# Typed attention pass of a graph network: one-hots on ScalarE, type masks built once, the next group's scores split around the totals

## The reference, cut to what matters

```python
k = typed_linear(x, Wk, bk); q = typed_linear(x, Wq, bq); v = typed_linear(x, Wv, bv)   # by node type, 4 heads
k_rel = einsum('nhd,rhde->rnhe', k, rel_att)      # 6 edge types
v_rel = einsum('nhd,rhde->rnhe', v, rel_msg)
att = (q[edge_dst] * k_rel[edge_type, edge_src]).sum(-1) * rel_pri[edge_type] / sqrt(dk)
seg = edge_dst * 6 + edge_type                    # a softmax for each destination and type
ex  = exp(att - segment_max(att, seg)[seg])
w   = ex / segment_sum(ex, seg)[seg]
hsum = segment_sum(w[:, :, None] * v_rel[edge_type, edge_src], seg)
```

## Time and profile before

| | |
|---|---|
| median of 3 runs | 8833.31 us (8825.69 to 8842.84) |
| profiled execution, span | 8830.1 us |
| mean granted TensorE clock over the span | 0.819 |
| TensorE matmul, busy | 6600.0 us (75%) |
| VectorE | 5164.4 us (58%) |
| GpSimd | 4060.3 us (46%) |
| ScalarE | 2234.7 us (25%) |
| typed pass, from 592 to 2110 us | 1518 us, of it VectorE 1309.29, TensorE 1098.34, GpSimd 817.01, ScalarE 353.68 |

### The profile page before, as it was taken

How to read it: one execution, slowest core, us unless ns; L and a number is a source line. 1 busy time by engine, 2 the same in 40 slices (tenths; PEclk the granted TensorE clock), 3 DMA queues, 4 the chain that set the end, 5 groups by cost and what they waited for, 6 DMA issues and landing times. The chain is left out here.

```text
span 8830.1 us, 116392 instructions
## 1 busy us (share of the span) xinstructions
PE 6600.0 (75%) x27378; PEld 5018.6 (57%) x27379; DVE 5164.4 (58%) x9644; ACT 2234.7 (25%) x4857; POOL 4060.3 (46%) x4373
## 2 busy tenths in 40 slices
PE   4977777774736666679999999974788885787886
PEld 2546566563525444546666666653676673666665
DVE  3138888886243333246666666665666666566666
ACT  1222222221310000123333333332333331333332
POOL 0025555552037777124444444423666661666663
PEclk9988888886857777589999999986777776677777
DMA  2247767666013333133343344332444441544443
GB/s 92 99 144 212 214 208 213 207 209 151 4 57 105 105 105 105 29 108 115 115 124 114 116 121 116 117 83 85 135 139 135 131 140 37 149 133 135 136 135 90
DMA packets 440058, 1096.42 MB, mean 124 GB/s; under 512 B 102452, under 2 KB 177296, under 8 KB 439410
## 3 DMA queue, kind: packets, MB, share of 16 engines
q0 software_dynamic: 249344, 763.23, 30.9%
q1 hardware_dynamic: 190180, 328.60, 11.1%
HBM read 1009.55 MB, written 81.94 MB: 124 GB/s over the span
## 5 line engine op out<-in xcount | busy, mean ns | idle before, releaser
L731 POOL DMA_INDIRECT st_rows<-g_table,st_stage_idx x1632 | 1558.0, 955 | 873.4 <-issue 463.6
L824 POOL DMA_INDIRECT st_rows<-kv_table,st_stage_idx x832 | 806.2, 969 | 671.1 <-PE st_psM L1167 391.2
L2385 PE MATMUL st_psM<-st_msg,st_hot 128*128 128x273 f32 x3264 | 942.6, 449 | 128.0 <-DVE st_msg L2233 102.6
L677 POOL DMA_INDIRECT st_rows<-p_table,st_stage_idx x816 | 854.3, 1047 | 302.9 <-issue 220.3
L731 POOL DMA_INDIRECT st_rows<-h_table,st_stage_idx x816 | 777.0, 952 | 244.5 <-issue 234.8
L2385 PEld LDWEIGHTS st_psM<-st_msg,st_hot 128*128 128x128 f32 x3264 | 702.9, 221 | 321.5 <-DVE st_msg L2233 91.2
L1519 DVE TENSOR_TENSOR st_pre<-st_psP,st_rows 128x512 f32<-128x512 f32 x816 | 523.5, 682 | 531.5 <-PE st_psP L1610 392.6
L1616 PE MATMUL st_psC<-st_w,st_rT 128*128 128x256 f32 x3264 | 814.7, 392 | 0.0
L1616 PEld LDWEIGHTS st_psC<-st_w,st_rT 128*128 128x128 f32 x3264 | 587.3, 190 | 373.7 <-ACT st_rT L1577 212.3
L1426 PE MATMUL st_psM<-st_rows,st_hot 128*128 128x256 f32 x1632 | 512.3, 484 | 372.5 <-DMA st_rows<-h_table,st_stage_idx 190.4
L1426 PEld LDWEIGHTS st_psM<-st_rows,st_hot 128*128 128x128 f32 x1632 | 401.3, 251 | 480.7 <-issue 331.3
(11 more groups left out here) (394 smaller groups left out, 11250.1 us busy)
## 6 DMA issues: line engine op xcount, KB each, us to landing
st_dst_row<-in_dst_row SPq DMA_DIRECT2D x310, 512.0 KB, 5.7
kv_table<-st_rows_out SPq DMA_DIRECT2D x25, 1560.0 KB, 5.7
st_ea<-in_ea SPq DMA_DIRECT2D x103, 256.0 KB, 3.8
st_rows<-g_table,st_stage_idx POOLq DMA_INDIRECT x1632, 2.8
st_pens<-pen_table SPq DMA_DIRECT2D x208, 72.0 KB
st_rows<-kv_table,st_stage_idx POOLq DMA_INDIRECT x832, 4.5
st_rows<-h_table,st_stage_idx POOLq DMA_INDIRECT x816, 2.7
st_rows<-p_table,st_stage_idx POOLq DMA_INDIRECT x816, 3.7
```

The lines of the kernel that those rows point to most:

```text
L677: pool.indirect_dma_start(out=rows[:, u * SLOTS + j, :], out_offset=None, in_=table, in_offset=bass.IndirectOffsetOnAxis(ap=stage_idx[:, u ...
L731: pool.indirect_dma_start(out=rows[:, slot, j, :], out_offset=None, in_=table, in_offset=bass.IndirectOffsetOnAxis(ap=stage_idx[:, g, u * ...
L824: pool.indirect_dma_start(out=rows[:, slot, j, :], out_offset=None, in_=kv_table, in_offset=bass.IndirectOffsetOnAxis(ap=stage_idx[:, g, u ...
L2385: last = nc.tensor.matmul(out[:, 0:MSG_W], onehots[:, j, :], msg[:, n, j, :], start=(j == 0), stop=(j == SLOTS - 1))
```

## The change

In the typed pass:

- `make_hot` moves from VectorE to ScalarE. It becomes, for each supertile, eight Squares of 128 columns (iota row plus a bias of minus the destination number, `minus_rel`), a wait for them, and one Relu of 1,024 columns. Its place is behind `make_extra_hotrows(q + 1, 1)`, ahead of `make_hotrow(q + 2, .)`.
- `mine` and `other` are made once for all slots, as 16-bit floats, in `typed_tables`, behind the preparation of the relation weights. `spread_types` keeps its four additions.
- `edge_scores(q + 1, 0)` is split: the first half of the slots comes between the maxima and the totals, the second behind the totals.
- `extra_hots` comes behind the messages.
- Both work tables hold 16-bit numbers; `prepare` writes `minus_rel` in one more instruction; some tiles move to other scopes; in `typed_tables` the type masks are made ahead of two fills.

```diff
@@ gnn
-    work = sb(top, "work", [1, NS + 2 * U + 2, 4], I32)
+    work = sb(top, "work", [1, NS + 2 * U + 2, 4], U16)
...
-    type_f = sb(early, "type_f", [P, NT + UT * SLOTS])
-    typed_rel = sb(early, "typed_rel", [P, NT])
-    typed_work = sb(early, "typed_work", [1, NS + 2 * U + 2, 4], I32)
+    minus_rel = sb(early, "minus_rel", [P, NT])
+    mine = sb(early, "mine", [P, NT + UT * SLOTS, RELS], BF16)
+    other = sb(early, "other", [P, NT + UT * SLOTS, RELS], BF16)
+    typed_work = sb(early, "typed_work", [1, NS + 2 * U + 2, 4], U16)
@@ prepare
+                    v.tensor_scalar(minus_rel[:, :], typed_rel[:, :], -1.0, None, ALU.mult)
@@ typed_tables, VectorE
+                    link.turn()
+                    wide = [P, NT + UT * SLOTS, RELS]
+                    link(v.tensor_tensor(mine[:, :, :], type_f[:, :].unsqueeze(2).to_broadcast(wide),
+                                         iota_row[:, 0:RELS].unsqueeze(1).to_broadcast(wide), ALU.is_equal))
+                    link(v.tensor_scalar(other[:, :, :], mine[:, :, :], -1.0, BIG, ALU.add, ALU.mult))
@@ typed_pass, VectorE
-                    def edge_scores(q, u, slot, turn):
+                    def edge_scores(q, u, slot, turn, halves=(0, 1)):
                         s = UT * q + u
-                        _, x1, _, _ = work_typed(dve, s + 1)
-                        typed_rows_in(dve, slot, turn)
-                        for h in range(2):
+                        if 0 in halves:
+                            _, x1, _, _ = work_typed(dve, s + 1)
+                            typed_rows_in(dve, slot, turn)
+                        for h in halves:
...
                     def spread_types(q):
-                        link(v.tensor_tensor(mine[:, :, :, :, :].rearrange("p u k j r -> p (u k j) r"),
...
-                        link(v.tensor_scalar(other[:, :, :, :, :], mine[:, :, :, :, :], -1.0, BIG, ALU.add, ALU.mult))
...
-                                    other[:, u, half, :, :].unsqueeze(2).to_broadcast(wide),
+                                    types_of(other, q, u, half),
...
                         link.turn()
-                        make_hot(q, 0)
                         segment_maxima(q)
-                        make_hot(q, 1)
+                        edge_scores(q + 1, 0, ahead_slot, ahead_turn, (0,))
                         segment_totals(q)
-                        edge_scores(q + 1, 0, ahead_slot, ahead_turn)
+                        edge_scores(q + 1, 0, ahead_slot, ahead_turn, (1,))
                         edge_weights(q)
                         for u in range(UT):
                             messages(slot + u, u)
+                        for u in range(UT):
+                            extra_hots(q, u)
                         link(edge_scores(q + 1, 1, ahead_slot + 1, ahead_turn))
                         spread_types(q + 1)
-                        for u in range(UT):
-                            extra_hots(q, u)
@@ typed_pass, ScalarE
+                    def make_hot(q, u):
+                        s = UT * q + u
+                        link.turn()
+                        act.wait_ge(S["summed"], START + s - 1)
+                        for j in range(SLOTS):
+                            last = nc.scalar.activation(hot[:, u, j, :], iota_row[:, :], ACT.Square,
+                                                        bias=minus_rel[:, ds(s * SLOTS + j, 1)])
+                        link(last)
+                        nc.scalar.activation(hot[:, u, :, :], hot[:, u, :, :], ACT.Relu, bias=ones_col[:, :],
+                                             scale=-1.0).then_inc(S["onehot"], 1)
...
                         make_extra_hotrows(q + 1, 1)
+                        for u in range(UT):
+                            make_hot(q, u)
                         for u in range(UT):
                             make_hotrow(q + 2, u, 16 * q + 48)
```

More of the change, by code:

```diff
@@ L22 @@
 I32 = mybir.dt.int32
+U16 = mybir.dt.uint16
 ALU = mybir.AluOpType
@@ L174, in gnn @@
     hidden = ExitStack()
+    type_f = sb(hidden, "type_f", [P, NT + UT * SLOTS])
     X = sb(hidden, "x_in", [P, NB, D])
@@ L196, in prepare @@
             first = st.sb("first", [P, NT])
+            typed_rel = st.sb("typed_rel", [P, NT])
             least = st.sb("least", [P, 2, NS])
@@ L593, in _ @@
                     link = Link(dve, S["link_dve"])
-                    link(v.memset(rows[:, :, 2 * D:KV_W], 0.0))
-                    for r in range(RELS):
-                        v.memset(rows[:, r, 2 * D + r:2 * D + r + 1], 1.0)
                     for t in range(TYPES):
@@ L602, in _ @@
                     last.then_inc(S["masks"], 1)
+                    link(v.memset(rows[:, :, 2 * D:KV_W], 0.0))
+                    for r in range(RELS):
+                        v.memset(rows[:, r, 2 * D + r:2 * D + r + 1], 1.0)
                     dve.wait_ge(S["rel_in"], 16 * 3 * H0)
@@ L774, in typed_pass @@
             att = st.sb("att", [P, UT, 2, HALF, H0])
-            mine = st.sb("mine", [P, UT, 2, HALF, RELS])
-            other = st.sb("other", [P, UT, 2, HALF, RELS])
             et = st.sb("et", [P, HALF, 2, UT, G])
@@ L789, in typed_pass, with types_of @@
             psM = [st.ps(f"psM{u}", [P, 512]) for u in range(UT)]
-            columns = psM[0][:, 512 - P:512]
+            def types_of(tile, q, u, half):
+                return tile[:, ds((UT * q + u) * SLOTS + half * HALF, HALF), :].unsqueeze(2).to_broadcast([P, HALF, H0, RELS])
             lanes = psX[0:T_LANES, :]
@@ L956, in spread_types @@
                     def spread_types(q):
-                        link(v.tensor_tensor(mine[:, :, :, :, :].rearrange("p u k j r -> p (u k j) r"),
-                                             type_f[:, ds(UT * q * SLOTS, UT * SLOTS)].unsqueeze(2).to_broadcast([P, UT * SLOTS, RELS]),
-                                             iota_row[:, 0:RELS].unsqueeze(1).to_broadcast([P, UT * SLOTS, RELS]), ALU.is_equal))
-                        link(v.tensor_scalar(other[:, :, :, :, :], mine[:, :, :, :, :], -1.0, BIG, ALU.add, ALU.mult))
                         wide = [P, HALF, H0, RELS]
@@ L965, in spread_types @@
                                     et[:, :, half, u, :].rearrange("p j (h r) -> p j h r", h=H0),
-                                    other[:, u, half, :, :].unsqueeze(2).to_broadcast(wide),
+                                    types_of(other, q, u, half),
                                     att[:, u, half, :, :].unsqueeze(3).to_broadcast(wide), ALU.add)
                         last.then_inc(S["scored"], 1)
-                    def make_hot(q, u):
-                        s = UT * q + u
-                        x0, _, _, _ = work_typed(dve, UT * q + 1)
-                        dve.wait_ge(S["summed"], START + s - 1)
-                        dve.wait_ge(S["opened"], START + UT * q - 1)
-                        dve.wait_ge(S["x_opened"], START + x0)
-                        one_hot(hot[:, u, :, :], typed_rel[:, ds(s * SLOTS, SLOTS)], columns).then_inc(S["onehot"], 1)
                     def extra_hots(q, u):
@@ L982, in extra_hots @@
                         with dve.If(more):
-                            link(v.tensor_copy(rel[:, :], typed_rel[:, ds(s * SLOTS, SLOTS)]))
+                            link(v.tensor_scalar(rel[:, :], minus_rel[:, ds(s * SLOTS, SLOTS)], -1.0, None, ALU.mult))
                             with dve.Fori(x0, x1) as x:
@@ L1021, in edge_weights @@
                                     totals[:, :, half, u, :].rearrange("p j (h r) -> p j h r", h=H0),
-                                    mine[:, u, half, :, :].unsqueeze(2).to_broadcast(wide),
+                                    types_of(mine, q, u, half),
                                     back_view()[:, :, at:at + G].rearrange("p j (h r) -> p j h r", h=H0), ALU.mult)
@@ L1051, in group @@
                             messages(slot + u, u)
+                        for u in range(UT):
+                            extra_hots(q, u)
                         link(edge_scores(q + 1, 1, ahead_slot + 1, ahead_turn))
                         spread_types(q + 1)
-                        for u in range(UT):
-                            extra_hots(q, u)
-                    v.tensor_copy(columns, iota_row[:, :])
                     link(v.tensor_reduce(pick[:, :], ident[0:T_LANES, 0:T_LANES].rearrange("p (c r) -> p c r", r=RELS),
```

## The result

The changed kernel takes 8856.47 us (median of 10 runs, 8843.46 to 8879.99), the kernel before 8833.05 in as many. The ratio is 1.0029, with a 95% interval of 1.0019 to 1.0038: slower by some 23 us, where 8707 was forecast. The profiled execution has a span of 8855.8 us, 25.7 more than before.

What follows compares the result with a forecast made beforehand. VectorE was taken to set the pace in the typed pass, with TensorE a close second. 50 groups times (29.05 - 26.5) gave 127 us, less 0.6, from the median 8833.3 to 8707; range 8645 to 8775.

Steps and rivals of the forecast that it cites:

- Part 5: GpSimd needs 21.1 us a group and fits; masks hidden; 16-bit loads taken at the same time, 16 us either way.
- Rival D: 16-bit row takes one load per number: 1.03 us more a read, later stages +245, typed pass +75, 9027 us; chance 0.05.
- Part 1: What leaves VectorE: scan starts at 0.95 us instead of 3.09, gain 2.1, second L715 1.14; register work hidden behind messages.
- Part 2: VectorE's new order in the typed pass: new 1.3 us wait ahead of L1020; VectorE alone gives 25.9 us a group.
- Part 3: TensorE's low-clock expansion holds the sums back 0.8 to 1.6 us, adding 0.3 to 1.1; 26.5 us a group taken.
- Rival A: The forecast: VectorE and TensorE set the pace by turns, 26.2 to 27.0 us a group, 8680 to 8735; chance 0.60.
- Part 4: ScalarE: a Square of 128 columns takes 0.3 us, one make_hot 3.7 us, ready before TensorE needs it; costs nothing.

Runs made afterwards that it cites:

- e1: The changed kernel with both work tables back at 32-bit numbers and the first two numbers of a row masked with 4095: 8709.37 us, ratio 0.9858.
- e2: The kernel before with both work tables of 16-bit numbers and nothing else: 9167.73 us, ratio 1.0377.
- e9: Reads alone, nothing of the network computed, twelve of each kind: on VectorE four 16-bit numbers took 0.945 us, four 32-bit ones 0.339.
- e11: e1 with half of the products of TensorE's expansion of (q+1, 1) left out: 8758.66 us, ratio 0.992.
- e3: The kernel before, 32-bit tables kept, with the first two numbers of each row read masked with 4095: 8902.60 us, ratio 1.008.
- e10: e1 with the mask made only where a number is used, and at the read on SyncE alone: 8685.78 us, ratio 0.9835.
- e6: The same kernel as e10, run on another chip where the kernel before takes 10386.75 us: ratio 1.007.

## Why the prediction was wrong

**The step that failed** is in Part 5: "No row shows a 16-bit load. I take the same time", with a tenth either way for its bounds. The read takes 2.76 times as long, 0.948 against 0.344 us. A price that no row showed was bounded by a tenth of its nearest row, though VectorE alone pays it 476 times outside the typed pass. Rival D had the place and almost the form: one load per number, 1.03 us more. The load stays one instruction and costs 0.60 more. Put through D's own sum: 238 exposed reads times 0.60 is 143 us (measured 126), and behind the messages 2.2 + 3 x 0.60 = 4.0 us fit under 4.53, so that only the bare one counts, 30 us in 50 groups (after less e1: 0.62 a group, 31). That gives 8707 + 143 + 30 = 8880, 24 over the measured 8856. The half that D took as exposed came near as a total only: VectorE's read is bare in all 102 supertiles of the edge network and costs nothing in the weighted sum. D's chance, 0.05, was too low. e1, e2 and e9 settle the cause: the type alone, put in or taken out, moves the edge network, the attention passes and the typed pass, and the read by itself has the same length. That e1, the change with its reads at the old price, takes 8709 us where 8707 was forecast is luck in part: its typed pass gained 138 us and its attention passes 30, its edge network and typed tables lost 51.

**Part 1: right.** The table loads of the extra ranges cost nothing behind the messages.

**Part 2: right, with one term missing.** Gap ahead of L1020 1.30 us, forecast 1.3. L999 stands 1.05 us behind the additions in e1 (1443.95 + 0.77 to 1445.77), forecast 0.95; in after 1.29. Missing is the bare read ahead of the first half of the scores: 0.72 us of gap a group with 16-bit reads, 0.22 with 32-bit ones (e1, masks and all). Part 1 rightly let VectorE's sequencer run four instructions ahead behind the messages. Between maxima and totals it can't, because it has just waited for the end of L1000. The trace of before shows the same read bare behind the totals (0.60 us ahead of L950, rows 3).

**Part 3: the mechanism right, its size too large.** The clock still falls, and TensorE's gap was 5.76 us in after and 4.88 in e1 (4.7 forecast). With 16-bit reads the sums are held 1.2 us. In e1 the low stretches are 6.8, 10.2 and 10.2 us long in turn, and in such three groups the sums start 2.58, 3.00 and 3.63 us after the messages, held 0.0, 0.4 and 1.1 us. The first and the last of them:

```profile
1436.99 7.33 PE L1178 MATMUL st_psM<-st_rows,st_hot 128*128 128x262 f32 x32
1444.87 0.61 PE L1203 MATMUL st_psX<-ident,st_et 128*96 128x128 f32 x4 [0.55 <-DVE st_et L972]
...
1490.37 7.23 PE L1178 MATMUL st_psM<-st_rows,st_hot 128*128 128x262 f32 x32
1497.43 0.60 PE L1203 MATMUL st_psX<-ident,st_et 128*96 128x128 f32 x4
```

In the first TensorE is done 0.55 us before VectorE's additions and delays nothing; in the last, held by a full 1.1 us, it starts them 0.4 us after the additions' end at 1497.05. The forecast let a hold of 0.8 to 1.6 us come in every group and pass on 0.3 to 1.1 of it. What passes on is bounded by L999's idle time, 1.10 us a group where 0.95 is bare latency: 0.15. With 25.9 us of VectorE alone, 26.22 leaves 0.3 for that, the bare read and the masks. Rival A's case is thus what the new order does, at its lower end: 50 x (29.10 - 26.22) = 144 us against 127 forecast.

The Trainium skill, "TensorE: Matmul & The Clock Gate", section "HAM oscillation", says that a recurring wait re-throttles the array in every round. The trace of after agrees: one fall in each of its groups. So does e11, where the longer low stretches take more time than eight products save.

**Part 4: right.** Square 0.305 us (0.3 taken), a one-hot 3.6 (3.7), ready 5.6 us ahead (5). The Trainium skill, "ScalarE: Activation LUTs", section "What ACT_TABLE_LOAD costs", states 280 ns plus 0.833 ns a column with a bias operand, less 93 ns back to back: an estimate of 0.29 us, with which the trace agrees within 5%.

**Part 5, the rest: right.** `mine` takes 5.35 us (5.9 taken) and `other` 1.46 (1.5 to 5.9), both hidden. From 750 to 1990 us of after VectorE never waits for gathered rows, so GpSimd kept up. Not forecast: the typed tables took 6 us more (497 instead of 491), at 410.4 us of busy TensorE from 150 to 590 us instead of 404.0. There are more single falls of the clock in that stretch. The change's own edits there aren't the cause: e3, which leaves this stage as before, takes 498 us with 410.4 busy.

**What stays open.** e1's attention passes are 12 and 18 us shorter than before's though its reads are no cheaper. In e3, which has the masks alone, they are 9 and 4 shorter. No run tells where this comes from. It also hides a part of the read's price: against e1 the 16-bit reads cost the two passes 45 and 51 us, not 33 each. 32-bit tables under the new order with no mask at all weren't tried.

## What to carry to other kernels

When a change touches the type or the layout of what sequencers read into registers, price the read on its own, in every stage that uses it: here 0.6 us a read undid, in stages that the change did not mean to touch, the whole gain of the stage that it did. A read is free where several microseconds of queued work stand ahead of it (here the messages), and bare where the engine has run out or its sequencer has just waited for the engine's own last instruction. So the 16-bit type cost 3.2 us a group in one order and 0.6 in another. And the more often a price that no row shows is paid, the wider its bound has to be.

## What the runs showed of the hardware that was not expected

- A register read of 16-bit numbers grows with their number (0.286, 0.503, 0.945 us for one, two, four on VectorE); of four 32-bit numbers it takes 0.339. In the kernel the four 16-bit ones take 0.987 us on TensorE's queue and 0.886 on ScalarE's.
- Less work on TensorE made the kernel slower: with 8 products fewer a group the granted clock stayed at 1.2 GHz for 13.6 us of each 27.3, and the sums took 9.29 us instead of 7.33.
- VectorE's sequencer gets no further ahead than its last wait for its own engine: behind four queued messages a read of 0.95 us is hidden, behind two short instructions 0.72 us of gap is left on average.
- The same kernel takes 8830 to 8833 us on the chips of the other runs and 10387 on one, where ScalarE stands idle for 90 us ahead of its Squares instead of 2, and an edit that gains 1.65% on the one (e10) loses 0.7% on the other (e6).
